# K projection moved behind the scores and transposes of its pair in the repeated self-attention order

## The reference, cut to what matters

```python
x = x + attn(layernorm(x), w_q, w_k, w_v, w_o)
# attn, per batch n and head h
q = einsum('ntc,hdc->nhtd', x_q, w_q)
k = einsum('ntc,hdc->nhtd', x_q, w_k)
v = einsum('ntc,hdc->nhtd', x_q, w_v)
a = einsum('nhtd,nhsd->nhts', q, k) / sqrt(64)
a = where(causal_forbidden, -inf, a)
y = einsum('nhts,nhsd->nthd', softmax(a, axis=3), v).reshape(n, t, -1)
return y @ w_o
```

## Time and profile before

| | us |
|---|---|
| median of three runs | 1494.63 (1492.79 to 1495.24) |
| profiled execution, span from first to last instruction | 1491.1 |
| PE busy in the span | 1472.1 (99%) |
| DVE busy | 1148.2 (77%) |
| ACT busy | 965.1 (65%) |
| POOL busy | 514.4 (34%) |
| stretch read for the six repeated periods | 90.6 to 668.2 |

### The profile page before, as it was taken

One profiled execution on the slowest core, in us unless ns is written; L12 is line 12 of the kernel. 1 busy time (PEld: TensorE's weight loads), 2 busy tenths in 40 slices (PEclk: granted clock), 3 DMA queues, 4 the chain that ended last, 5 costly groups with the idle time before them and its releaser, 6 DMA issues.

```text
span 1491.1 us, 29084 instructions
## 1 busy us (share of the span) xinstructions
PE 1472.1 (99%) x10536; PEld 1247.0 (84%) x10536; DVE 1148.2 (77%) x2904; ACT 965.1 (65%) x2262; POOL 514.4 (34%) x787
## 2 busy tenths in 40 slices
PE   8999999999999999999998999999999999999999
PEld 6888888888888888888887788888888888888887
DVE  7999999999999999999999677777875634444442
ACT  6988888888888888888887854556555532222222
POOL 2545655546546555555453011000110211111110
PEclk9999999999999999999999999999999999999999
DMA  5000101001001010010012433343323532222221
GB/s 156 2 1 2 58 2 36 24 2 58 1 16 44 1 58 2 9 50 2 23 65 91 169 120 121 113 142 127 119 95 109 197 106 85 85 86 86 86 86 43
DMA packets 69274, 99.74 MB, mean 67 GB/s; under 512 B 5376, under 2 KB 46720, under 8 KB 69120
## 3 DMA queue, kind: packets, MB, share of 16 engines
q1 hardware_dynamic: 69120, 97.69, 19.4%
HBM read 62.02 MB, written 35.65 MB: 65 GB/s over the span
## 4 chain that ended last, share of the span: by engine, by line
PE 91%; DVE 4%; ACT 2%; DMA 2%; issue 1%; SPq 0%; POOL 0%; DVEq 0%
PE bank L1088 15%; PE bank L1090 13%; PE bank L681 10%; PE bank L601 9%; PE bank L653 8%; PE bank L603 7%; PE bank L602 7%; PE bank L665 6%; PE bank L1247 2%; PE bank L1238 2%; PE bank L1096 2%; PE bank L1214 2%; PE bank L1205 2%; PE bank L1203 2%; PE bank L1207 2%; DVE PT L751 1%
## 5 line engine op out<-in xcount | busy, mean ns | idle before, releaser
L872 POOL TENSOR_SCALAR P<-P,stats 128x512 f32<-128x512 f32 (+3 forms) x512 | 268.9, 544 | 329.7 <-DVE stats L850 329.6
L737 ACT ACTIVATE P<-P,stats 128x384 f32<-128x384 f32 (+3 forms) x512 | 284.0, 560 | 17.3 <-DVE stats L842 17.1
L704 ACT ACTIVATE PT<-bank 128x512 fp32r<-128x512 f32 (+1 forms) x384 | 185.4, 525 | 86.6 <-PE bank L665 85.5
L842 DVE CUSTOM_DVE_ANT_0 P<-bank,cmask 128x384 f32<-128x384 f32 (+3 forms) x512 | 228.4, 483 | 1.1 <-PE bank L653 0.9
L751 DVE TENSOR_TENSOR PT<-bank,PT 128x512 fp32r<-128x512 f32 (+1 forms) x384 | 218.5, 594 | 4.9 <-ACT PT L704 4.1
L1409 DVE TENSOR_TENSOR Hb<-gt,Hb 128x512 fp32r<-128x512 f32 x128 | 90.7, 709 | 166.3 <-ACT Hb L1255 164.8
L1088 PE MATMUL bank<-Hb,hw 128*128 128x512 f32 x512 | 201.2, 393 | 0.8 <-DVE Hb L1409 0.8
L1088 PE MATMUL bank<-w,hw 128*128 128x512 f32 x512 | 199.2, 389 | 0.0
L681 PEld LDWEIGHTS bank<-PT,V 128*128 128x128 f32 x1024 | 165.1, 190 | 22.9 <-DVE PT L751 4.3
L681 PE MATMUL bank<-PT,V 128*128 128x512 f32 (+3 forms) x1024 | 176.1, 319 | 3.5 <-DVE PT L751 3.5
L1090 PE MATMUL bank<-Hb,hw 128*128 128x512 f32 x448 | 174.6, 390 | 0.0
(11 more groups left out here) (237 smaller groups left out, 3322.7 us busy)
## 6 DMA issues: line engine op xcount, KB each, us to landing
h_scratch<-go SPq DMA_DIRECT2D x64, 256.0 KB, 2.0
xs<-x_scratch SPq DMA_DIRECT2D x23, 512.0 KB, 4.2
hx<-h_scratch SPq DMA_DIRECT2D x32, 256.0 KB, 6.1
stageA<-in_h SPq DMA_DIRECT2D x14, 512.0 KB, 4.0
x_scratch<-x SPq DMA_DIRECT2D x8, 512.0 KB, 3.5
x_scratch<-xs SPq DMA_DIRECT2D x8, 512.0 KB, 3.6
qf<-h_scratch SPq DMA_DIRECT2D x16, 256.0 KB, 5.0
pf<-h_scratch SPq DMA_DIRECT2D x16, 256.0 KB, 5.7
```

Source lines behind the costliest of these rows:

```text
L704: return e.activation(dst, src, ACT.Copy, scale=scale)
L737: e.activation(p, p, ACT.Exp, bias=st_[:, k:k + 1], scale=-1.0, accum_out=st_[:, 8 + k:9 + k]).then_inc(s_exp, 1)
L842: e.tensor_tensor_reduce(P_tile(P, i, a), banks["S", P, max(i, 1)][a][:, slice(*S_COLS[i])], cmask[:, 512 - n:512], -1.0, 3.0e38, ALU.add, ...
L872: e.tensor_scalar(p, p, stats[P % 4][:, k:k + 1], 1.0, ALU.mult, ALU.mult).then_inc(s_norm, 1)
```

## The change

Only TensorE's row of `BATCH` changes. In each of the eight pairs of a period, the step `k` moves behind the last `S` or `T` of the group of two or three in which it stood. Nothing is added or taken away, and the tables of the other engines, `HEAD` and `TAIL` stay.

```diff
-        S:0:2 T:-1:0 S:0:1 k:1 T:-1:1 O:-2 AV:-1:0 q:1 AV:-1:1 v:3 T:0:2 S:1:3 S:1:2 T:0:1 k:2 S:1:1 T:0:0 q:2
+        S:0:2 T:-1:0 S:0:1 T:-1:1 k:1 O:-2 AV:-1:0 q:1 AV:-1:1 v:3 T:0:2 S:1:3 S:1:2 T:0:1 S:1:1 T:0:0 k:2 q:2 O:-1
...
```

More of the change, by code:

```diff
@@ L67 @@
     "PE": """
-        S:0:2 T:-1:0 S:0:1 k:1 T:-1:1 O:-2 AV:-1:0 q:1 AV:-1:1 v:3 T:0:2 S:1:3 S:1:2 T:0:1 k:2 S:1:1 T:0:0 q:2
[L69 to L73, removed]
+        S:0:2 T:-1:0 S:0:1 T:-1:1 k:1 O:-2 AV:-1:0 q:1 AV:-1:1 v:3 T:0:2 S:1:3 S:1:2 T:0:1 S:1:1 T:0:0 k:2 q:2 O:-1
+        AV:0:0 AV:0:1 v:4 T:1:2 S:2:3 S:2:2 T:1:0 S:2:1 T:1:1 k:3 O:0 AV:1:0 q:3 AV:1:1 v:5 T:2:2 S:3:3 S:3:2 T:2:0
+        S:3:1 T:2:1 k:4 q:4 AV:2:0 v:6 AV:2:1 O:1 T:3:2 S:4:3 S:4:2 T:3:0 T:3:1 S:4:1 k:5 q:5 AV:3:0 v:7 AV:3:1 O:2
+        T:4:2 S:5:3 S:5:2 T:4:0 S:5:1 T:4:1 k:6 q:6 v:8 AV:4:0 AV:4:1 O:3 T:5:2 S:6:3 S:6:2 T:5:0 T:5:1 S:6:1 k:7 v:9
+        q:7 AV:5:0 AV:5:1 O:4 T:6:2 S:7:3 S:7:2 T:6:0 T:6:1 S:7:1 k:8 q:8 AV:6:0 AV:6:1 v:10 O:5 T:7:2 S:8:3""",
     "ACT": """
```

## The result

The changed kernel takes 1560.92 us (median, 1557.77 to 1562.56), the kernel before, run beside it, 1494.93. The ratio is 1.0445, with a 95% interval of 1.0429 to 1.0461: 66.0 us slower. Forecast were 1553.5 us and a range of 1537 to 1572; the narrower range of the case that was summed, 1544 to 1559, was passed by 2 us.

The account below looks back on a forecast made before the run. PE was taken to bound the kernel, gapless in the repeated periods. The groups' terms sum to 9.8 us a period, six times 58.9, taking the profiled 1491.1 to 1550.0 and the median to 1553.5 us; range 1537 to 1572.

Parts of the forecast that it names:

- the case that was summed: Waits, late K and saved width changes add to 9.8 us a period: 1553.5 us, own range 1544 to 1559, chance 0.80.
- The bound: PE, busy 1472.1 of 1491.1 us, has no gap in the repeated periods; each us it waits there counts whole.
- Changes of width: On PE, switches between 64-row and 128-row work: fewer per pair, saving 0.28 us each, 2.24 in a period.
- Waits ahead of the second transposes and scores: PE waits for VectorE's readers to free banks: 0.67 to 1.51 us at seven places; k:4 instead +1.35 net.
- The release: Time from a reader's end to the waiting matmul: taken as 0.06 us, at most 0.10.
- The hand-off: Later K delays kh, kl and pl, so the next AV waits: 1.35 us at k:3, 0.43 at k:2, 0.10 at k:4.
- the lateness handed on: VectorE begins the group of k:5 late after k:4, costing 0.54 us.
- the lower bound: ScalarE and VectorE work off small backlogs while PE waits, and k:5's 0.54 may be absorbed: 8.2 us a period, +49.
- only the changes of width count: Rival: VectorE frees the banks early enough, so 13.4 us are gained: 1481 us, chance 0.05.
- the hand-off alone: Rival: banks free in time, but the chain through kh and kl stays: 2 us gained, 1492.5, chance 0.06.
- all eight groups pay for a late kh: Rival: work for the next AV ends behind a late kh everywhere: 112 us slower, 1607; chance 0.09 including the clock.
- The clock: Rival: TensorE falls to 1.2 GHz in the new waits, costing up to twice the step; counted within the 0.09.

Follow-up runs that it names:

- short m in the old order: Kernel before, VectorE's m of pairs 6 to 63 handling only the first 128 columns, the others left out: 1493.22 us, ratio 0.9992.
- k:8 with the short m: Changed kernel, m of pairs 6 to 63 cut to 128 columns, kh and kl of pairs 2 to 4 moved behind ph and pl: 1496.68 us.
- experiment 3: Changed kernel, with kh of pairs 2, 3 and 4 moved behind ph and kl of pairs 3 and 4 behind pl: 1548.08 us, ratio 1.0363.
- the five groups without hand-off: Kernel before, with only k:1, k:5, k:6, k:7 and k:8 moved: 1519.45 us, ratio 1.0166.
- experiment 4: Changed kernel, with kh and kl of pairs 3 and 4 moved behind ph and pl, those of pair 2 left: 1547.33 us, ratio 1.0347.
- experiment 5: Changed kernel's order, but each step writes to the PSUM banks it had in the kernel before: 1558.80 us, ratio 1.0438.
- experiment 9: Changed kernel, kh and kl moved behind ph and pl, VectorE doing first in each group the readers PE waits for, complete work: 1513.10 us, ratio 1.0128.

## Why the prediction was right

**The bound.** PE without a gap, so that each us of waiting counts in full: right. The short m in the old order left every group where it was.

**Changes of width.** 0.28 saved for a pair: the two parts of 0.10 are seen in the steps of the timeline after, and 0.21 of it came out as a gain at k:8 with the short m.

**Waits ahead of the second transposes and scores.** Right in mechanism in all eight groups. At k:3 and k:6 a part of the wait sits ahead of the scores and is for a pl, which the prediction says of k:3 alone. VectorE's reader ended when it was expected in k:1 to k:4, to 0.01 us, and in k:6 to 0.05. The release was not as expected: 0.06 was taken from reader's end to matmul, and at k:3 it is 0.11 behind the m (441.95 to 442.06) and 0.14 behind the pl (440.74 to 440.88). The bound of 0.10 was too small as well: it came from a place where PE hardly waited. At k:3 this is 0.05 ahead of the transposes and 0.09 ahead of the AV product, which then takes 0.08 longer: 0.22 of the 0.25 by which the group lost more than forecast. k:2, with two such waits, lost 0.26 more.

**The hand-off.** Right: 1.35 forecast at k:3, and experiment 3 took 1.53 away there (2.46 to 0.93), at k:5 0.39 of the lateness handed on (0.54 forecast). At k:4 it was priced too low: 0.10 forecast, 0.33 taken away by experiment 3 (1.72 to 1.39), and the 0.23 between them are most of the 0.27 by which that group came out above its forecast. At k:2 0.43 was forecast and 0.61 to 0.65 measured, from the periods without a fall of the clock (1.90 to 1.25 or 1.29).

**The size.** 58.9 was forecast, 66.0 measured, 63.9 of it in the stretch. The mis-sized term is the release of a waiting matmul and what PE needs to start again. Two smaller ones are the hand-off at k:4 and k:7, 0.65 instead of 0.39: in that group VectorE's m ends 3.40 us after the first transposes (of T:5:2), where it ended 3.22 after them before, because VectorE, held up by the late K of k:6, reaches vl 0.18 later. That lateness and the 0.09 of release make up the 0.26; the prediction had taken VectorE's start there as unchanged. k:8 was too dear by 0.12: its m ends 0.20 sooner after the group's first transposes than before, a backlog as the lower bound named it. k:5 was too dear by 0.10, since k:4 handed on less than the 0.54. So two groups came out below the forecast by 0.2 together and six above it by 1.1, and a part of the nearness of the sum is this.

**The rivals.** That only the changes of width count (1481), or the hand-off alone with them (1492.5), is excluded by the five groups without hand-off: +25 us. That all eight groups pay for a late kh (1607) is excluded by the table. The clock, counted as a part of that rival with the remark that nothing shows a fall in waits so short, did fall in experiments 3, 4 and 5, after waits of 1.5 to 1.6 us; in the changed kernel it did not in the repeated periods.

## What to carry to other kernels

A step that looks misplaced between two others can be the cover under which another engine empties the banks that the next step needs: before it is moved, work out when the step behind it could start and when its banks are free. Here, on an engine that never waited, a move cost the difference of these two at each place, and the places could be summed but for 0.2 to 0.4 us that some of them handed on to the next. And where an operand is made later, look in the other engines' queues for what stands behind its copy; here it was 1.53 of the 2.46 us of the worst group, and moving two entries took it away.

## What the runs showed of the hardware that was not expected

**The clock fell after a wait of 1.5 us.** In the profiled execution of experiment 3, three of the six periods, and four of six in experiment 4, show a fall of TensorE's granted clock at the same place, in the group of k:2. In experiment 5 one period of six shows one at k:4, where the scores had waited 1.6 us for a pl; the group lost 2.88 instead of 1.61 to 1.67. Stretches around one of them, in experiment 3 (the granted clock is the mean of each stretch):

```profile
417.00:422.70 5.70, 4.79 (x58) 3.86 (x56) 4.60 (x13) 3.42 (x9) 3.10 (x6) 1.00 0.00 0
422.70:426.10 3.40, 2.99 (x22) 2.44 (x23) 3.28 (x12) 1.78 (x4) 0.00 (x0) 0.72 0.01 2
426.10:433.00 6.90, 6.90 (x39) 6.18 (x38) 4.28 (x14) 5.32 (x16) 2.95 (x6) 0.89 0.01 2
```

and PE's rows there:

```profile
420.89 0.90 PE L645 MATMUL bank<-K,Q 64*128 64x256 f32 x12
423.11 0.71 PE L657 MATMUL bank<-ident,P 64*128 64x64 f32 x16 [1.32 <-DVE stats L834]
423.75 0.50 PE L593 MATMUL bank<-XT,Wk 128*128 128x512 f32 x1
424.08 0.52 PE L594 MATMUL bank<-XT,Wk 128*128 128x512 f32 x1
424.40 0.63 PE L595 MATMUL bank<-XT,Wk 128*128 128x512 f32 x1
424.83 0.63 PE L593 MATMUL bank<-XT,Wk 128*128 128x512 f32 x1
```

Ahead of the fall PE waited 1.5 us for the m; 1.3 us after it began again, the steps of its projection take 0.43 us (424.40 to 424.83) instead of 0.23, that is from the level of 2.4 GHz to that of 1.2 GHz, and the group loses 1.1 to 1.6 us more than the same group in a period without a fall. The changed kernel has the same wait in all six periods, and in its profiled execution the clock fell at none. What decides between the periods stays open; no run here varies it. The Trainium skill, "TensorE: Matmul & The Clock Gate", HAM oscillation, tells of a kernel that loses the clock in each wait for a transfer; these rows show it after a wait for another engine, shorter than the ones described there.

**A matmul behind a wait starts later after its releaser, and runs longer.** In the changed kernel's repeated periods, a matmul that stood idle for a reader on VectorE starts 0.11 us after that reader's end at the second transposes of k:1, k:2 and k:3, and 0.15 at the ten other places, the same in all six periods to 0.01. What decides between the two is open: 0.11 and 0.15 are both found behind an m. Where the inputs came just in time it was 0.10 (417.60 to 417.70), and in experiment 9 the projections that had waited at most 0.2 us started 0.06 after an m. An AV product takes 1.30 from its start to the next step after such a wait and 1.22 without.
